# Middle token stages by seven products, with three halves quantised in each of two weight stages

## The reference

```python
# x (32, 128, 2048) = 4096 token rows; weight, W_base (2048, 2048)
lora_delta = lora_B @ lora_A * 0.5
normalized = (weight + lora_delta).reshape(O, I // 128, 128) / exp(scale_log)
quantized = cb[searchsorted(thresholds, normalized, side='left')]      # 32 levels
w_eff = (quantized * scale).reshape(O, I) + lora_delta
h = x @ w_eff.T
result = h @ W_base.T + b_base
ax, probs = h @ A_w.T, softmax(h @ router_w.T)                        # 16 and 8 columns
mixed = einsum(einsum(ax, cores), probs)
out = x + result + (mixed @ B_w.T) * 2
```

## Time and profile before

| | before |
|---|---|
| median of 3 runs | 2352.81 us (2351.86 to 2354.84) |
| the profiled execution | 2352.95 us, span 2351.2 us |
| TensorE busy | 2281.0 us, 97% |
| VectorE busy | 1846.1 us, 79% |
| ScalarE busy | 1464.8 us, 62% |
| POOL busy | 1288.8 us, 55% |
| transfers | 459.6 MB, queue busy 57.3% |

### The profile page before, as it was taken

How to read it: one execution, slowest core, us unless ns; L and a number is a source line. 1 busy time by engine, 2 the same in 40 slices (tenths; PEclk the granted TensorE clock), 3 DMA queues, 4 the chain that set the end, 5 groups by cost and what they waited for, 6 DMA issues and landing times.

```text
span 2351.2 us, 31846 instructions
## 1 busy us (share of the span) xinstructions
PE 2281.0 (97%) x11778; PEld 2083.8 (89%) x11778; DVE 1846.1 (79%) x2363; ACT 1464.8 (62%) x1926; POOL 1288.8 (55%) x792
## 2 busy tenths in 40 slices
PE   3989899999999999999999999999999999999999
PEld 2445479999999989999999989999999999999998
DVE  8999998889978866777777976777775666777776
ACT  8999978889877655666665665666663665121221
POOL 6888846669764336666663335666662222232331
PEclk9999999999999999999999999999999999999999
DMA  6788854453334335676674334666666666556463
GB/s 210 262 284 280 312 199 164 164 176 136 145 134 133 116 98 190 230 240 226 221 243 149 115 102 162 227 232 228 241 204 208 186 195 202 206 200 235 189 225 153
DMA packets 133088, 459.63 MB, mean 195 GB/s; under 512 B 14098, under 2 KB 66898, under 8 KB 96082
## 3 DMA queue, kind: packets, MB, share of 16 engines
q1 hardware_dynamic: 132932, 457.59, 57.3%
HBM read 306.41 MB, written 151.13 MB: 195 GB/s over the span
## 4 chain that ended last, share of the span: by engine, by line
PE 91%; DVE 6%; ACT 2%; DMA 1%; issue 1%; DVEq 0%; SPq 0%; ACTq 0%
PE m L970 15%; PE m L969 15%; PE m L971 15%; PE m L926 5%; PE m L927 5%; PE m L925 5%; PE m L868 5%; DVE acc L1362 4%; PE m L1018 4%; PE m L1020 4%; PE m L1019 4%; PE m L956 2%; PE m L957 2%; PE m L958 2%; ACT mk L1131 1%; PE pd L1018 1%
## 5 line engine op out<-in xcount | busy, mean ns | idle before, releaser
L1362 DVE SCALAR_TENSOR_TENSOR acc<-mk,dj,acc 128x1024 f32<-128x1024 uint8 x736 | 945.4, 1285 | 102.8 <-ACT mk L1131 83.6
L1131 ACT ACTIVATE mk<-wr,bj 128x1024 uint8<-128x1024 f32 x736 | 809.0, 1139 | 1.0 <-DVE acc L1362 0.5
L970 PE MATMUL m<-gl,xh 128*128 128x384 f32 (+2 forms) x1920 | 674.1, 351 | 0.0
L969 PE MATMUL m<-gh,xh 128*128 128x384 f32 (+2 forms) x1920 | 673.5, 351 | 0.0
L971 PE MATMUL m<-gh,xl 128*128 128x384 f32 (+2 forms) x1920 | 671.6, 350 | 0.0
L1606 POOL TENSOR_TENSOR pp<-pp,tm 128x1024 f32<-128x1024 f32 x184 | 447.3, 2431 | 22.3 <-POOL tm L1592 0.6
L971 PEld LDWEIGHTS m<-gh,xl 128*128 128x128 f32 x1920 | 360.6, 188 | 18.0
L969 PEld LDWEIGHTS m<-gh,xh 128*128 128x128 f32 x1920 | 361.0, 188 | 17.2
L970 PEld LDWEIGHTS m<-gl,xh 128*128 128x128 f32 x1920 | 360.9, 188 | 16.9
L1592 POOL TENSOR_SCALAR tm<-mp,dj 128x1024 f32<-128x1024 uint8 x192 | 217.6, 1134 | 281.5 <-ACT mp L1137 276.3
L1413 DVE TENSOR_TENSOR kl<-kw,kh 128x416 fp32r<-128x416 f32 (+3 forms) x310 | 238.0, 779 | 104.9 <-ACT kh L1165 103.7
(11 more groups left out here) (198 smaller groups left out, 3363.7 us busy)
## 6 DMA issues: line engine op xcount, KB each, us to landing
part<-part SPq DMA_DIRECT2D x192, 1036.0 KB, 7.6
rows<-in_wb SPq DMA_DIRECT2D x61, 1036.0 KB, 4.8
out<-part SPq DMA_DIRECT2D x31, 1024.0 KB, 4.5
kw<-in_ws SPq DMA_DIRECT2D x128, 208.0 KB, 2.6
xw<-in_x SPq DMA_DIRECT2D x96, 256.0 KB, 3.4
kw<-in_wb SPq DMA_DIRECT2D x92, 192.0 KB, 2.4
wr<-in_w SPq DMA_DIRECT2D x32, 512.0 KB, 8.6
dl<-delta SPq DMA_DIRECT2D x30, 512.0 KB, 5.9
```

The costliest lines, as they stand in the source:

```text
L969: e.matmul(R.m[c][:, 0:w], xh, gh, start=k == 0, stop=False)
L970: e.matmul(R.m[c][:, 0:w], xh, gl, start=False, stop=False)
L1131: e.activation(R.mk[m % NM], w, ACT.Identity, bias=R.bj[:, j:j + 1], scale=GROW).then_inc(S["mk"], 1)
L1362: e.scalar_tensor_tensor(R.acc, R.mk[m % NM], R.dj[:, j:j + 1], R.acc, ALU.mult, ALU.add).then_inc(S["ac"], 1)
```

## The change

In the token stages of groups 1 and 2 the tiles go in pairs. Pairs 0 and 15 are multiplied by chunks as before. In pairs 1 to 14 ("mixed"), columns 0 to 447 of each half (SW = 448) go by seven products of two half-size blocks each, on sums of token blocks and of G blocks, and the remaining 588 columns of each half by three pieces of 392 ("rest"), one of which is 196 columns of either half. The sums of G (`spread`) are built in pair 0 of the stage by VectorE, ScalarE and POOL, the token sums by POOL (`token_sums`) one pair ahead. There are four token buffers for three. The seven products share banks 0 (products 1, 6, 7, 4) and 1 (2, 5, 3) and each is added to its part of the partial sum; the rests rotate over four banks.

The quantisation is spread otherwise: 3 halves in each of the two G stages and 5 in each of the two token stages, for 2 and 6. In the token stages it starts 9 units of work later and ends 11 earlier. In the G stages POOL makes the low part of every fourth slot. The splits of the weight halves move to the last pair of the token stage, and to slots 20 to 32 of the last weight stage; VectorE makes six of the low halves.

```diff
-UNTIL_TOKENS, UNTIL_WEIGHTS = (16, 24, 32), (0, 18, 26, 32)
+UNTIL_TOKENS, UNTIL_WEIGHTS = (16, 24, 32), (0, 19, 27, 32)
+SW = 448
+REST = (HX - SW) // 3 * 2
+MIX = (("prod", 1), ("prod", 2), ("rest", 0, 0), ("rest", 0, 1), ("prod", 6), ("prod", 5), ("rest", 0, 2), ("prod", 7),
+       ("prod", 3), ("rest", 1, 0), ("prod", 4), ("rest", 1, 1), ("rest", 1, 2))
+VECTOR_SPLITS = (17, 19, 21, 23, 25, 27)
+WAIT_LEVELS, END_LEVELS, WAIT_SLOTS = 9, 11, 4
+LATE_HALF = {1: 19, 2: 27}
+def mixed_tokens_of(g, back):
...
+    for k, u in enumerate(UNITS_OF[g]):
+        p, at = u[0], k - PAIR_FIRST[g][u[0]]
+        yield ("mul", g, k)
+        if at == 0:
+            yield ("fetch", g, p)
+        if p == 0 and at in (0, 1, 2):
+            yield ("spread", g, at)
...
+        if p + 1 < PAIRS:
+            if at == 3:
+                yield ("x_split", g, 2 * p + 2)
+            if at == 4:
+                yield ("x_split", g, 2 * p + 3)
+                yield ("more", g, p)
+            if at == 5 and mixed(p + 1):
+                yield ("token_sums", g, p + 1)
...
+            if at == 9 and mixed(p + 1):
+                yield ("token_sums_high", g, p + 1)
+                yield ("token_sums_low", g, p + 1)
...
+        elif at < 7:
+            if g + 1 < LAST or at < 4:
+                yield ("split", SPLITS[g + 1][at])
+        if at == (9 if mixed(p) else 5):
+            yield ("half_done", g, p)
...
+        passed += costs[k]
+        yield from back.levels(until, min(1.0, max(0.0, passed / total)), 0)
+def unit_bank(u):
+    if u[1] == "chunk":
+        return u[3]
+    if u[1] == "prod":
+        return 1 if u[2] in (2, 3, 5) else 0
+    return 2 + (6 * u[0] + 3 * u[2] + u[3]) % 4
+def low_on_pool(g, s):
+    return g in MIXED and s % 4 == 3
+        elif what == "fetch":
+            g, p = at
+            if p + 1 < PAIRS:
+                load_x(g, 2 * p + 2)
+                load_x(g, 2 * p + 3)
+            if p:
+                store_part(g, 2 * p - 1)
+        elif what == "more":
+            g, p = at
+            if p:
+                load_part(g, 2 * p + 2)
+        elif what == "half_done":
+            g, p = at
+            store_part(g, 2 * p)
+            if p + 1 < PAIRS:
+                load_part(g, 2 * p + 3)
+            elif g == 1:
+                raw(2 * FIRST[LAST])
+    def mul(g, k):
...
+        before = bank_before(g, k)
+        if before is not None:
+            e.wait_ge(S["ed"], added(g, before))
...
+            for kp in range(2):
+                high, low = sum_factor(g, p, n, kp)
+                oh, ol = sum_operand(n, kp, False), sum_operand(n, kp, True)
+                e.matmul(bank[:, 0:SW], high, oh, start=kp == 0 and n in (1, 2, 5), stop=False, skip_group_check=n in (3, 4, 6, 7))
+                e.matmul(bank[:, 0:SW], high, ol, start=False, stop=False, skip_group_check=n in (3, 4, 6, 7))
+                done = e.matmul(bank[:, 0:SW], low, oh, start=False, stop=kp == 1, skip_group_check=n in (3, 4, 6, 7))
+        else:
...
+            for b in range(GROUP[g]):
+                r = slice(b * 128, (b + 1) * 128)
+                gh, gl = rest_columns(R.gh[b], i), rest_columns(R.gl[b], i)
+                e.matmul(rest_bank(bank, i), xh[:, r], gh, start=b == 0, stop=False)
+                e.matmul(rest_bank(bank, i), xh[:, r], gl, start=False, stop=False)
+                done = e.matmul(rest_bank(bank, i), xl[:, r], gh, start=False, stop=b == GROUP[g] - 1)
+    def spread(g, k):
...
+        if k == 0:
+            e.wait_ge(S["used"], NS * g)
+            e.wait_ge(S["lo"], NCH * FIRST[g + 1])
+            rebuilt(1, 0, 1)
+            rebuilt(0, 0, 0)
+            e.wait_ge(br, n + 2)
+            e.tensor_tensor(f[0], r[1], r[0], ALU.subtract).then_inc(br, 1)
...
         elif what == "slot":
             g, s = at
-            if s + AHEAD < slots_of(g):
+            if s + AHEAD < slots_of(g) and not low_on_pool(g, s + AHEAD):
                 weight(g, s + AHEAD)
+    def weight(g, s):
+        w = slot_width(g, s)
+        e.wait_ge(S["gh"], NS * (g - 1) + s + 1)
+        kw, kl, kh = R.ring(s)
+        e.tensor_tensor(kl[:, 0:w], kw[:, 0:w], kh[:, 0:w].bitcast(F32), ALU.subtract).then_inc(S["gq"], 1)
```

More of the change, by code:

```diff
@@ L161, in weights_of @@
             yield ("x_split", g, 1)
-        yield from back.levels(until, min(1.0, (s + 1) / (NS - 6)), 2 * FIRST[g])
+        wait = WAIT_SLOTS if g - 1 in MIXED else 0
+        yield from back.levels(until, min(1.0, max(0, s + 1 - wait) / (NS - 6 - wait)), 2 * FIRST[g])
 def tokens_of(g, back):
@@ L233, in walk @@
             yield from weights_of(g, back)
-        if g < LAST:
+        if g in MIXED:
+            yield from mixed_tokens_of(g, back)
+        elif g < LAST:
             yield from tokens_of(g, back)
@@ L444, in wait_final_row, with mixed, units_of_stage, unit_columns @@
         e.wait_ge(S[f"f{k}"], 16)
+def mixed(p):
+    return MIX_FIRST <= p <= MIX_LAST
+def units_of_stage():
+    units = []
+    for p in range(PAIRS):
+        if mixed(p):
+            units += [(p, *u) for u in MIX]
+        else:
+            units += [(p, "chunk", u, c) for u in range(2) for c in range(NCH)]
+    return units
+def unit_columns(u):
+    if u[1] == "prod":
+        return 6 * SW
+    return 12 * (REST if u[1] == "rest" else width(u[3]))
+def unit_bank(u):
+    if u[1] == "chunk":
+        return u[3]
+    if u[1] == "prod":
+        return 1 if u[2] in (2, 3, 5) else 0
+    return 2 + (6 * u[0] + 3 * u[2] + u[3]) % 4
@@ new lines, in last_unit, with first_unit, prod_unit, multiplied @@
+def last_unit(g, t, reads):
+    return max(k for k, u in enumerate(UNITS_OF[g]) if u[0] == t // 2 and t % 2 in unit_tokens(u)[reads])
+def first_unit(g, t, reads):
+    return min(k for k, u in enumerate(UNITS_OF[g]) if u[0] == t // 2 and t % 2 in unit_tokens(u)[reads])
+def prod_unit(g, p, n):
+    return PAIR_FIRST[g][p] + MIX.index(("prod", n))
+def multiplied(g, k):
+    return MC_BASE[g] + k + 1
+def added(g, k):
+    return ED_BASE[g] + k + 1
+def bank_before(g, k):
+    return max((j for j in range(k) if unit_bank(UNITS_OF[g][j]) == unit_bank(UNITS_OF[g][k])), default=None)
@@ new lines, in target_before, with sums_count, sums_free, x_buffer @@
+def target_before(g, k):
+    p, kind, *at = UNITS_OF[g][k]
+    same = [j for j in range(PAIR_FIRST[g][p], k) if UNITS_OF[g][j][1] == "prod" and TARGET[UNITS_OF[g][j][2]] == TARGET[at[0]]]
+    return max(same, default=None)
+def sums_count(g, p):
+    return NMIX * (g - 1) + p - MIX_FIRST + 1
+def sums_free(g):
+    return multiplied(g, prod_unit(g, MIX_LAST, 3))
+def x_buffer(g, t):
+    return t % 4 if g in MIXED else t % 3
+def x_landed(g, t):
+    if g == 0:
+        return 16 * (t // 3 + 1)
+    k = t % 4
+    return 16 * ((PER_SLOT[k] if k < 3 else 0) + NT // 4 * (g - 1) + t // 4 + 1)
@@ L447, in wait_evacuated, with x_released, rest_columns, rest_bank @@
+def x_released(g, k):
+    if g == 0:
+        return NCH * (3 * (PER_SLOT[k] - 1) + k + 1)
+    return multiplied(g, last_unit(g, NT - 4 + k, 1))
+def rest_columns(t, i):
+    if i < 2:
+        return t[:, HX * i + SW:HX * i + SW + REST]
+    return halves(t)[:, :, SW + REST:HX]
+def rest_bank(bank, i):
+    return bank[:, 0:REST] if i < 2 else halves(bank[:, 0:REST])
+def both_blocks(t, i, h):
+    return t.rearrange("p (a i n) -> p a i n", a=2, i=2)[:, :, i, HX * h:HX * h + SW]
 def wait_evacuated(e, S, g, t, c):
-    if g == 0 and c in ACT_CHUNKS:
+    if g in MIXED:
+        e.wait_ge(S["ed"], added(g, PAIR_FIRST[g][t // 2] + NCH * (t % 2) + c))
+    elif c in ACT_CHUNKS:
@@ L669, in store_part @@
     def store_part(g, t):
-        for c in range(NCH):
-            wait_evacuated(e, S, g, t, c)
+        if g == 0:
+            for c in range(NCH):
+                wait_evacuated(e, S, g, t, c)
+        else:
+            e.wait_ge(S["ed"], added(g, last_unit(g, t, 0)))
         e.dma_start(part[t], R.part[t % 3]).then_inc(S[f"po{t % 3}"], 16)
@@ L745, in sync_program @@
             q, j = at
-            if j == 0 and 2 * N0 < q + 1 < NQ:
+            if j == 0 and 2 * N0 < q + 1 < NQ and q + 1 not in (24, *LATE_HALF.values()):
                 raw(q + 1)
@@ L802, in sync_program @@
                     weight(g + 1, s)
+        elif what == "late_half":
+            raw(LATE_HALF[at[0]])
+        elif what == "fetch":
[16 more added lines that the diff above has]
+                raw(2 * FIRST[LAST])
+        elif what == "next_weights":
+            for s in range(RING):
+                weight(at[0] + 1, s)
         elif what == "close":
@@ L1294, in scalar_program @@
                 weight(g + 1, 1)
+        elif what == "next_rounded":
+            weight(at[0] + 1, 0)
+            weight(at[0] + 1, 1)
+        elif what == "spread_high":
+            spread_high(*at)
+        elif what == "token_sums_high":
+            token_sums_high(*at)
         elif what == "close":
@@ L1530, in vector_program @@
```

(19 more changed lines are left out.)

261 lines of the change are left out of this document (226 added, 35 removed), and 3 rows, old and new, of the table COMPUTE.

## The result

The changed kernel took 2357.81 us (median of 17 runs, 2354.87 to 2360.00); the kernel before, in 17 runs on the same chip, 2352.81 us. The ratio is 1.0021, with a 95% interval of 1.0014 to 1.0027: some 5 us slower, where 18 us less was forecast. The profiled execution has a span of 2354.9 us for 2351.2.

The account below looks back on a forecast made before the run. TensorE, busy without a gap in the G and middle token stages, was taken to bound the kernel. 2352.95 - 34.2 (term 1) + 14.2 (term 2) + 2 (term 3) = 2335 us, range 2317 to 2352.

Parts of the forecast that it names:

- Term 1: Middle token stages: seven products and rests need 2,688 fewer columns per mixed pair at 0.4550 ns each, 34.2 us less.
- The matmuls cost more than their columns: Rival, token stages: dearer 196-wide pieces give 2341 us, or shared banks holding up TensorE 2355; chance 0.08.
- term 3: Token stages: VectorE's work fits, tight bank reuse costs 2 us (0 to 10), moved background work costs nothing.
- Term 2: G stages: VectorE's low parts wait longer for POOL, stalling 6.0 and 6.2 us; POOL's low parts add 2: 14.2 us.
- The prediction's formula: G stages, first 48 slots: VectorE's time from instruction prices plus w per low part, against TensorE's 100.4 us in stage 1.
- The G stages keep up: Rival: VectorE's waits for POOL stay at 0.41 to 0.55 us, neither G stage is late, 2321 us; chance 0.27.
- The G stages eat the gain: Rival, first 48 slots of both G stages: w from 1.05 loses the gain, 1.3 gives 2368 us; chance 0.12.
- The partial sums come late: Rival, token stages: store then load into one buffer delays additions and TensorE, 35 us, giving 2370 us; chance 0.05.

Follow-up runs that it names:

- e1: The changed kernel with the token stages' levels beginning 14 units of work into the stage instead of 9: 2337.18 us, 0.9937 of the kernel before.
- e6: e5 with the four late splits of the last weight stage 10 slots apart instead of 4: 2329.69 us, 0.9902 of the kernel before.
- e5: e1 with the G stages' levels spread by the columns of the slots instead of by their number: 2331.65 us, 0.9910 of the kernel before.
- e8: e1 with POOL's mask sums of halves quantised in the G stages cut from 1024 to 64 columns, for timing only: 2326.22 us, 0.9892.
- e2: The changed kernel with POOL's normalisation of half 19 or 27 put before the first token sums and token tile's low part: 2350.92 us, 0.9994.

## Why the prediction was wrong

**Term 1, the products (-34.2): right.** e1's token stages are 345.4 and 345.3 us for a forecast of about 345 each and up to 2 more. 0.455 ns a column holds for 448, for 392 and for the rest read as 2 x 196. "The matmuls cost more than their columns" is refuted for the rate; its second half, the shared banks, is part of term 3.

**Term 3, the token stages (+2, 0 to 10): in its range but for the heads.** Beside the two stalls at the head, the token stages of the kernel after are 5.2 us above their columns (11.2 + 12.0 - 18.0). Of these 3.6 are five waits for additions at a product, the kind of place that the prediction named, and 1.0 two short waits for a token tile's low part, which e1 has too.

**The step that failed** is the last sentence of term 3: "Normalisations moved to the stage's head, the W sums (in pair 0, needed by product 6 of pair 1, 29 us later), token sums on POOL (14 us ahead of use) and the moved splits (in the last pair, those of odd halves needed only at slot 8) cost nothing: each lies beside TensorE's chunks with that much time." It gave each piece of moved work its own slack and never added them up on POOL. There they stand in one queue: 9.3 us of low parts, 3 of token sums, 1.3 of a tile's low part, 4.3 of normalisation, the first not before 901.2, as POOL waited for VectorE's G sums until then, and with 1.1 us of another such wait between. That puts the end of the normalisation at 920.2, and VectorE's first level was due at 911.2, with additions behind it for which TensorE waited. It cost 9.3 and 8.7 us in the two stages, 18.0 in all, where the sum had nothing; e1 gave back that and the five short waits, 20.6 us in the medians and 22.3 in the two stages. A granted clock of half behind a stall was no term of the sum either: it is a quarter of that cost. (The expectation of e1 puts the cost at 20.6 us, as it counts the whole of the 6.8 us at half clock as time in which TensorE worked; the near agreement with the median is chance.)

**The moved splits** probably weren't free either. TensorE waits 4.3 us for low parts in the last weight stage for 1.4 before, and setting the splits apart took 1.2 us off that wait and 2.1 off the stretch (e6 against e5). The whole last stretch is 3.8 us longer; of this 2.9 is that wait, and the rest has no named releaser.

**Term 2, the G stages (+14.2): 12.7 in sum, but by errors that cancel.** w, the mean wait of a low part, was taken as 0.75 in both. By groups of VectorE's low parts in the kernel after, over the first 100 us of G stage 1 and 106 us of G stage 2:

```profile
L1797 DVE TENSOR_TENSOR kl<-kw,kh 128x384 fp32r<-128x384 f32 x32 | 32.8, 1026 | 0.8 <-ACT kh L1486 0.8
...
L1797 DVE TENSOR_TENSOR kl<-kw,kh 128x384 fp32r<-128x384 f32 x33 | 38.6, 1171 | 3.2 <-ACT kh L1486 3.1
```

Less the 0.55 of an undisturbed one, w is 0.48 and 0.62. The prediction's formula is not at fault: with 0.48 it has VectorE at 98.8 of 100.4 us in G stage 1, no stall, and the trace shows none for VectorE; with 0.62 it has G stage 2 5.2 us late and 3.1 after the lead, and TensorE waits 2.7 us for the G low parts. What was mis-sized was the growth of w in proportion to POOL's busy time: POOL was busy for 75.6 us in those 100.4, as forecast (73), yet w rose by a sixth in one stage and by half in the other. Most of the 9 us that VectorE did not cost was lost elsewhere: TensorE waited 5.6 us for POOL's own low parts where 2 (0 to 8) stood in the sum, 0.4 us went to a last addition, 1.7 to the clock in G stage 2, which is at 0.50 for 3.4 us, and 2.3 us are in no line of the waits. Of these some 1.3 go with the eight waits themselves: counted from start to start each is 0.16 us longer than its idle time, because the records of successive matmuls overlap by that much. The worst of POOL's low parts is the one that the prediction pointed out, behind `effective` of half 16; it was 2.2 us late for a forecast of 0.6, as the effective weight itself waited for VectorE. POOL's timeline:

```profile
761.68 1.90 POOL L2010 TENSOR_TENSOR wr<-wr,sc 128x1024 f32<-128x1024 f32 x1 [5.06 <-DVE wr L1707]
763.66 2.58 POOL L2012 TENSOR_TENSOR wr<-wr,dl 128x1024 f32<-128x1024 f32 x1
766.19 1.32 POOL L2088 TENSOR_TENSOR kl<-kw,kh 128x384 fp32r<-128x384 f32 x1
```

**The rivals.** *The G stages keep up* (2321): not so, but e5 to e8 show how near it was. *The G stages eat the gain* (2368): no, w stayed under the 1.05 from which it decides. The time is on that side for another reason. *The partial sums come late* (2370): refuted. Landings in token stage 1 after, 950 to 1200 us, loads and then stores of partial sums, beside the earlier trace rows:

```profile
DMA to landing us min/median/max: 4.7/4.9/5.7
...
DMA to landing us min/median/max: 3.9/4.3/9.0
```

A store and a load together take 9.2 us by the medians, for 16.7 with both in flight at once; the budget was 18.9.

**The account.** -34.2 of columns, +18.0 at the heads of the token stages, +5.2 elsewhere in them, +12.7 in the G stages, +3.8 behind them, -1.7 ahead of the first G stage: +3.8, against 3.7 us of span. The last term is no effect of the change as far as the traces tell: the first G stage begins at 709.8 us before and anywhere from 707.5 to 712.3 in the traces of the changed kernels, which all do the same up to there.

## What to carry to other kernels

Work that is moved off an engine must be added up in the queue that it lands in, in order and with the time at which its first input exists: three kinds of work, each with microseconds of slack, stood ahead of a fourth and made it 9 us late. An in-order engine that waits for a background result blocks the urgent instructions behind it, so the first consumer of moved work is the thing to place, and moving it later by five units (e1) was worth more than the one reordering of the producer that was tried (e2). Where TensorE is the bound, the price of a stall of several microseconds is to be taken with the half-clock stretch behind it, here 2.6 and 2.0 us on 6.7.
